# Moving one projection, its copies and one bias row between slots of an attention pipeline written out by hand

## What is computed

```python
q = jnp.einsum('bse,hde->bhsd', x, Wq) + bq[None, :, None, :]
k = jnp.einsum('bse,hde->bhsd', x, Wk) + bk[None, :, None, :]
v = jnp.einsum('bse,hde->bhsd', x, Wv) + bv[None, :, None, :]
causal = jnp.triu(jnp.ones((s, s), bool), 1)
scores = jnp.einsum('bhsd,bhtd->bhst', q, k) / scale
scores = jnp.where(causal[None, None], -jnp.inf, scores)
att = jax.nn.softmax(scores, axis=-1) / scale
z = jnp.einsum('bhst,bhtd->bhsd', att, v)
return z.reshape(b, s, h * dh) @ proj
```

## Time and profile before

| | |
|---|---|
| three runs, us | 1174.82, 1176.15, 1178.11 |
| median, us | 1176.15 |
| profiled execution: its time, its span, us | 1174.82, 1173.0 |
| TensorE busy, share of the span | 91% |
| VectorE, ScalarE, GpSimd busy | 66%, 61%, 46% |
| mean granted TensorE clock (1 is full) | 0.956 |
| first attention, units 0 to 15 | about 40 to 600 us of the span |

### The profile page before, as it was taken

One profiled execution on the slowest core, in us unless ns is written; L12 is line 12 of the kernel. 1 busy time (PEld: TensorE's weight loads), 2 busy tenths in 40 slices (PEclk: granted clock), 3 DMA queues, 4 the chain that ended last, 5 costly groups with the idle time before them and its releaser, 6 DMA issues.

```text
span 1173.0 us, 16993 instructions
## 1 busy us (share of the span) xinstructions
PE 1071.4 (91%) x5839; PEld 584.6 (50%) x5839; DVE 770.1 (66%) x1547; ACT 719.8 (61%) x1173; POOL 541.1 (46%) x446
## 2 busy tenths in 40 slices
PE   4699999999999999999956799999999579999998
PEld 2445555455455545555536422222322258778876
DVE  5767877777787777777545322225221379999998
ACT  4345555555565565555422499998999466666663
POOL 1356666666656666666630000000000126788786
PEclk9789999999999999999976699999999879999999
DMA  4111111111111111110200000000000002112110
GB/s 123 27 26 37 43 33 37 43 32 31 44 43 26 44 43 26 37 44 20 64 0 1 3 8 12 12 12 9 10 11 10 10 0 93 58 69 76 67 54 37
DMA packets 35290, 40.30 MB, mean 34 GB/s; under 512 B 19652, under 2 KB 22484, under 8 KB 34188
## 3 DMA queue, kind: packets, MB, share of 16 engines
q1 hardware_dynamic: 35212, 39.30, 13.0%
HBM read 19.23 MB, written 1.11 MB: 17 GB/s over the span
## 4 chain that ended last, share of the span: by engine, by line
PE 59%; DVE 27%; issue 9%; SPq 1%; ACT 1%; POOL 1%; DMA 1%; DVEq 0%; ACTq 0%; POOLq 0%
PE banks L1003 10%; PE banks L400 8%; PE banks L991 6%; PE banks L345 5%; PE banks L385 5%; DVE qb L1308 5%; PE banks L321 5%; PE banks L386 4%; PE banks L421 3%; PE banks L366 3%; DVE kb L581 2%; DVE banks L601 2%; DVE qa L581 2%; DVE zz L630 2%; DVE qb L610 2%
## 5 line engine op out<-in xcount | busy, mean ns | idle before, releaser
L710 POOL TENSOR_TENSOR pacc<-pacc,prob 128x1024 f32<-128x1024 f32 (+3 forms) x160 | 274.0, 1712 | 64.4 <-ACT prob L512 55.1
L1012 ACT ACTIVATE prob<-banks 128x1024 f32<-128x1024 f32 x256 | 238.7, 1094 | 22.1 <-PE banks L991 22.1
L512 ACT ACTIVATE prob<-banks 128x512 f32<-128x512 f32 (+3 forms) x384 | 167.8, 488 | 113.4 <-PE banks L386 111.8
L1341 POOL TENSOR_TENSOR ka<-prob,qb 128x512 fp32r<-128x512 f32 x108 | 165.0, 1549 | 59.6 <-ACT qb L1291 33.1
L385 PE MATMUL banks<-qa,ka 128*128 128x512 f32 (+3 forms) x384 | 150.7, 400 | 1.3 <-ACT prob L512 1.3
L400 PE MATMUL banks<-prob,v 128*64 128x512 f32 (+3 forms) x768 | 145.0, 498 | 1.0 <-POOL prob L701 1.0
L1297 ACT ACTIVATE prob<-banks,w 128x512 f32<-128x512 f32 x144 | 94.7, 687 | 71.3 <-PE banks L1259 71.3
L1003 PE MATMUL banks<-prob,v 128*32 128x512 f32 x1024 | 137.1, 608 | 0.8 <-DVE pacc L1020 0.3
L386 PE MATMUL banks<-qb,kb 72*128 72x512 f32 (+3 forms) x384 | 131.5, 350 | 0.0
L957 POOL TENSOR_TENSOR sq<-sq 64x512 f32<-64x512 f32 x8 | 8.3, 1033 | 261.3 <-DVE sq L953 261.3
L701 POOL TENSOR_SCALAR_AFFINE_SELECT prob<-prob 128x256 f32<-128x256 f32 x128 | 52.1, 407 | 147.6 <-ACT prob L512 145.9
(11 more groups left out here) (211 smaller groups left out, 1610.7 us busy)
## 6 DMA issues: line engine op xcount, KB each, us to landing
qb<-qa SPq DMA_DIRECT2D x64, 128.0 KB, 2.3
ka<-ka SPq DMA_DIRECT2D x64, 128.0 KB, 2.3
prob<-gate_rows SPq DMA_DIRECT2D x8, 1024.0 KB, 4.7
w<-in_experts SPq DMA_DIRECT2D x9, 514.0 KB, 3.5
wqkv<-in_wqkv SPq DMA_DIRECT2D x16, 193.0 KB, 2.4
x<-in_x SPq DMA_DIRECT2D x4, 256.0 KB, 4.1
zz<-pacc SPq DMA_DIRECT2D x64, 16.0 KB
wpr<-pacc SPq DMA_DIRECT2D x64, 16.0 KB
```

The source lines that it names most:

```text
L512: act.activation(pr[:, j % NRING, h, 0:wd], banks[:, h, 0:wd], ACT.Exp, scale=SCALE0).then_inc(s_exp, 1)
L710: pool.tensor_tensor(pacc[:, sbk, :, o:BLK], pacc[:, sbk, :, o:BLK], pr[:, j % NRING, :, 0:wd], ALU.add).then_inc(s_padd, 1)
L1012: act.activation(prob[:, n % NP1, :], banks[:, 2 * (n % 3):2 * (n % 3) + 2, :].rearrange("p b c -> p (b c)"), ACT.Exp, scale=2 * SCALE1).t ...
L1341: pool.tensor_tensor(act2[1][:, tb % 2, i, :], hid[:, tb % 2, i, :], act2[0][:, tb % 2, i, :], ALU.subtract).then_inc(s_hlP, 1)
```

## The change

In slots 7 to 11 TensorE's pieces for the next unit are placed anew. The two products with v of slots 4 and 5 go ahead of the projection of q (second half) instead of behind both projections; the projection of k goes one slot later, behind the scores of slot 8. The runs 3 and 4 of the maxima go one slot later each. Run 5 goes from behind the scores of slot 10 to behind those of slot 11, and v's projection goes ahead of run 6. ScalarE's rounding of k (second half) goes behind the exponential of slot 8, and VectorE's remainders and maxima follow. In slots 1 and 2 VectorE's order changes from maxima row, remainder of q, remainder of k to remainder of q, maxima row, remainder of k. No instruction is added or removed, none changes its shape, and no buffer changes.

```diff
@@ unit0_pe
                 elif j == 7:
+                    pv_pe(pe, u, w, 4, first)
+                    pv_pe(pe, u, w, 5, first)
                     if not last:
                         qk_pe(pe, n, x_, bn, 2, False)
-                        qk_pe(pe, n, x_, bn, 3, False)
-                    pv_pe(pe, u, w, 4, first)
-                    pv_pe(pe, u, w, 5, first)
                 elif j == 8 and not last:
-                    max_pe(pe, n, x_, 3)
+                    qk_pe(pe, n, x_, bn, 3, False)
                 elif j == 9:
                     pv_pe(pe, u, w, 6, first)
                     pv_pe(pe, u, w, 7, first)
                     if not last:
-                        max_pe(pe, n, x_, 4)
+                        max_pe(pe, n, x_, 3)
                         turn_pe(pe, n, 0, False)
                 elif j == 10 and not last:
-                    max_pe(pe, n, x_, 5)
+                    max_pe(pe, n, x_, 4)
                 elif j == 11:
+                    if not last:
+                        max_pe(pe, n, x_, 5)
                     pv_pe(pe, u, w, 8, first)
                     pv_pe(pe, u, w, 9, first)
                     if not last:
+                        v_pe(pe, n, x_, bn, 0)
                         max_pe(pe, n, x_, 6)
-                        v_pe(pe, n, x_, bn, 0)
@@ unit0_act
                 elif j == 7 and not last:
                     hi_act(act, n, x_, 2)
+                elif j == 8 and not last:
                     hi_act(act, n, x_, 3)
@@ unit0_dve
                 elif j == 1:
                     max_dve(dve, u, 9, first)
+                    if not last:
+                        lo_dve(dve, n, x_, 0)
+                elif j == 2:
                     mrow_dve(dve, u, w)
-                elif j == 2 and not last:
-                    lo_dve(dve, n, x_, 0)
-                    lo_dve(dve, n, x_, 1)
+                    if not last:
+                        lo_dve(dve, n, x_, 1)
...
                 elif j == 8 and not last:
                     lo_dve(dve, n, x_, 2)
+                elif j == 9 and not last:
                     lo_dve(dve, n, x_, 3)
                     max_dve(dve, n, 3, False)
-                elif j == 9 and not last:
+                elif j == 10 and not last:
                     max_dve(dve, n, 4, False)
-                elif j == 10 and not last:
+                elif j == 11 and not last:
                     max_dve(dve, n, 5, False)
-                elif j == 11 and not last:
                     max_dve(dve, n, 6, False)
```

## The result

The changed kernel is slower. Four runs have a median of 1188.1 us (1184.49 to 1189.48), beside 1175.49 us for four of the kernel before. Over all comparable runs of both, fifteen of the changed kernel among them, the ratio is 1.0088, with a 95% interval of 1.0067 to 1.0108, some 10 us. The profiled execution took 1183.85 us, with a span of 1182.1: 9.0 us over the profiled execution before.

What follows compares the result with a forecast made beforehand. TensorE bounds the units. Terms -0.44 + 0.22 + 0.17 + 0.51 give +0.46 us for fourteen units, +0.5 in unit 0: +6.9 on 1174.82, 1181.7, or 1183.1 as median; predicted 1181.5, range 1175.5 to 1186.5.

Steps and rivals of the forecast that it cites:

- Slower, by VectorE's order in slots 1 and 2: VectorE's first piece there waits for ScalarE's copy of q, so z and the output projection come 0.51 us later a unit.
- the alternation: VectorE, slots 1 and 2: remainders and maxima row interleaved, costed at nothing; another 0.1 us between instructions only as upper end.
- -0.44 + 0.22 + 0.17: Slots 7 to 11, a unit: 0.44 us gained before the projection, 0.22 lost at slot 9's scores, 0.17 at v's projection.
- The wait of slot 9's scores: TensorE waits for slot 8's exponential, queued on ScalarE behind the copy of q: 0.22 us a unit, bounds 0 and 0.45.
- The 0.17 at v's projection: v's projection followed by a run of the maxima instead of scores: 0.17 us more a unit, ends 0 and 0.24.
- Cover of runs 4 and 5: Slots 9 to 11: both runs of the maxima fit without waiting, run 5 by 0.3 us, so costed at nothing.
- the middle terms: The 0.22 at slot 9's scores and 0.17 at v's projection, held more likely too large than too small.
- (a): Rival: new TensorE gaps at slot 9's scores and v's projection do not appear; unit +0.07 us, 1176.3 us, no change; chance 0.20.
- (b): Rival: copy of q ready when VectorE finishes run 9; unit gains 0.32 us, 1170.3 us; chance 0.08.
- (c): Rival: longer waits at run 5 or slot 9's scores, or costly VectorE alternation; unit +0.85 us, 1187.2 us; chance 0.07.
- The rule on weight loads: Skill rule at TensorE's group boundaries: one group more would cost 0.19 us a unit, 2.7 us; not counted, a row contradicts it.

Runs made afterwards that it cites:

- experiment 7: Changed kernel with VectorE's old order in slots 1 and 2, v's projection behind run 6, both ScalarE copies behind slot 8's exponential; ratio 1.0052 to the kernel before.
- experiment 3: Changed kernel with VectorE's old order in slots 1 and 2 and v's projection behind run 6 of the maxima again; ratio 0.9981 to the kernel before.
- experiments 5: Changed kernel, old VectorE order in slots 1 and 2, v's projection behind run 6, both projections behind slot 8's scores, copies behind its exponential, run 5 apart; 1174.73 us, one execution.
- experiment 9: Changed kernel with output projection and run 1 of the maxima behind slot 6's scores, run 2 behind slot 7's; ratio 1.0003 to the kernel before.
- experiment 2: Kernel before with only VectorE's order in slots 1 and 2 changed, remainder of q ahead of the maxima row; ratio 1.0064 to the kernel before.
- experiment 4: Changed kernel, old VectorE order, v's projection behind run 6, both projections behind slot 8's scores, copies behind its exponential, runs 5 and 6 together; ratio 0.9856 to before.
- experiment 6: Kernel before with run 5 of the maxima moved from behind slot 10's scores to right ahead of run 6; ratio 1.0017 to the kernel before.
- experiment 8: Kernel before with only the products of slots 4 and 5 ahead of both second-half projections, copies together; 1205.49 us, one execution, beside 1174.79 for the kernel before.

## Why the prediction was right, and where its sizes were off

*Slower, by VectorE's order in slots 1 and 2.* Right, and shown from both sides: that edit alone has the loss, and without it there is none. The rule used was that a chain of waits without a break has no slack. The term was 0.51 us and measured 0.57. The remainder of q starts 2.58 us after its projection (226.84 to 229.42), where the maxima row started 2.13 after it (224.58 to 226.71): 0.45, for VectorE starts 0.03 us after ScalarE's end (229.39 to 229.42) and not the 0.1 I took. The other 0.12 is the alternation, which I had put at nothing and kept as an upper end. From the first of the three pieces to the Newton step it is 4.40 us (229.42 to 233.82) against 4.28: the maxima row, 1.28 us long, was followed after 1.21 by the remainder of q, and is followed after 1.32 by that of k (230.96 to 232.28). Before, on VectorE:

```profile
227.92 1.50 DVE L581 SCALAR_TENSOR_TENSOR qa<-banks,wqkv,qa 64x512 fp32r<-64x512 f32 x2
```

The Trainium skill has a rule for it ("VectorE: DVE Perf Modes", section "Two Vector instructions with no wait between them"): in its model, an instruction is held until all earlier ones have ended if an input starts in another group of 32 partitions than the first input last read from the same memory, or its output in another than the last one written there. The first instruction of the remainder of q reads from partition 0 and writes from partition 64, as the maxima row had done; that of k writes from partition 0, and the trace agrees with which of the two overlaps (1.21 and 1.32 behind a pair of 1.28). No experiment tested this rule apart from the order.

*The unit's second half, -0.44 + 0.22 + 0.17.* The sum was -0.05 and measured -0.05 in the unit shown (-0.02 to -0.05 over the units), but two of its terms were wrong and offset each other. I had taken a projection as half of a pair that is followed by products with v. With slot 8's scores it takes 1.91 us (209.84 to 211.75) and not 2.10 (0.955 + 1.14), with slot 9's, where they do not wait, 1.65 (experiment 7) and not 1.93 (0.955 + 0.97). The wait of slot 9's scores, which I put at 0.22, cost 0.69 by experiment 7. Only the end of the stretch hit, at 6.43 us (207.66 to 214.09) where I had 6.44. That is not only luck. Where the scores wait, their start hangs on ScalarE, the copy of q and then the exponential. I had it 5.44 us after the last matmul of slot 7's scores (205.37 to 210.81), and it came at 5.40 (207.66 to 213.06); what TensorE saves ahead of that point goes into the wait. The 0.17 at v's projection was right by experiment 3.

*Cover of runs 4 and 5.* Neither waits in the changed kernel. The margin of 0.3 us for run 5 was as thin as stated: experiments 5 and 7 overdrew it.

*The sum.* Fourteen units at 0.54 and unit 0 at 0.6 are 8.2 us; I had 6.9 in the sum and then took 5.3 over the median, on the guess that the middle terms were too large. That guess was the step that failed; the sum as it stood was nearer. The two traces differ by 9.1 us: the 8.2, the dip of 3.1, less 1.6 behind the stage and some 0.5 by which TensorE was ahead in unit 0 (its long wait there begins at 55.06 us and before at 55.54). The causes of these two small ones are open. I named no rival for the clock, since it was full in the units' rows that I had read. Whether the dip also makes the rest of the 10 us between the executions timed is open, as only one of them has a trace. The median of the four runs beside the kernel before lies 1.6 us above my range, the median of all fifteen, 1185.91 us, within it.

*The rivals.* (a), no new gaps: fallen, the gaps are there. (b), a copy ready in time: it ends at 229.39 (228.01 + 1.38), and VectorE had then been free for 0.9 us. (c), still slower by waits at run 5 or by alternation: the alternation was real, 0.12 a unit, the wait at run 5 was not there. So the direction and the largest term were right by their mechanism, and the small total of the second half by an offset.

*The rule on weight loads.* By it the one further group would have cost 0.19 us a unit and the second half would have come out at +0.14. It came out at -0.05, which alone is weak, since two terms of that sum were wrong. The row that speaks against it stands in the changed kernel too: the weight load of L386 starts 0.11 us after the matmul L385 (206.85) that lasts 0.50.

```profile
206.96 0.19 PEld L386 LDWEIGHTS banks<-qb,kb 72*128 72x128 f32 x1
```

## What to carry to other kernels

Where the chain of waits lies on one engine without a break up to the instruction that the bounding engine waits for, do not let its first piece wait for anything later, even if the total work is the same; or put another group in front of the waiting instruction, as experiment 9 did. A projection moved to fill a wait brings its eviction with it: look at what stands behind that eviction in the other engine's queue, and at who needs its result. Compare orders by the length of a repeated unit in the profile, since a lower granted clock moved the whole time here by 3 us (unit 15) to 6 us (the start of experiment 2), as much as 0.2 to 0.4 us in each of fourteen units.

## What the runs showed of the hardware

- Matmuls on 64 rows of the array cost by the group: two of 512 columns take 0.43 us, four in a row 0.66 (experiment 4) and 0.67 (experiment 6).
- What two fp32 projections take up to the next group depends on that group: 1.91 us ahead of products with v (206.14 to 208.05), 1.82 ahead of the turning of the maxima (224.58 to 226.40). In experiment 4 two of them and slot 9's scores take 2.52 us, where 2.88 had been read from the other order, 0.06 of it a wait.
- A stretch with several short waits can be followed by one at half the clock although TensorE is busy in most of both: 2.64 of 3.10 us busy, then 3.2 us at 1.2 GHz, every third unit in experiment 7 and eight of thirteen units in experiment 8. The same wait of 1.59 us at the end of the stage was followed by a dip in the changed kernel's trace and by none in that of the kernel before.
- A VectorE pair of 1.28 us was followed by the next pair after 1.21 us where that one wrote from the same partition, and after 1.32 us where it did not.
